# Masks of the first score block in quadrants, the mean's term and the constant rows on GpSimd, and new orders of work

## The chip, the cores and the metric

The kernel runs on one NeuronCore of a Trainium2 chip. The metric is the device time of one execution in microseconds (us). Five engines run their own instruction lists, each strictly in order, and meet only in semaphores: TensorE (PE in the profile, its weight loads PEld), VectorE (DVE), ScalarE (ACT), GpSimd (POOL) and SyncE (SP), which here only issues DMA transfers.

## The reference, cut to what matters

The input is x of shape 8 x 512 x 256: eight batches of 512 tokens. Each token is normalized, and two branches are added to x:

```python
xn = (x - mean(x)) / sqrt(var(x) + 1e-5)
# attention: 16 heads of 16, each token sees itself and the 63 before it
q, k, v = split(xn @ Wq), split(xn @ Wk), split(xn @ Wv)
attn = softmax(q . k_window / 4)            # tokens before the start are masked
a = (attn . v_window) @ Wo
# feed-forward with ternary weights (-1, 0, 1 by a threshold on |W|)
h = gelu(xn @ ternary(W_fc).T)              # 512 x 1024, exact gelu
h = (h - mean(h)) * rsqrt(var(h) + 1e-5) * ln_w + ln_b
f = h @ ternary(W_proj).T
out = x + a + f
```

## The kernel before, in words

All products run in fp16 or bf16 with each fp32 operand split into an upper and a lower half (`_hi`, `_lo`): ACT writes the upper half while it reads PSUM, DVE subtracts it from the PSUM value to get the lower. The second normalization is not applied to h. Instead the product of the raw gelu with `ln_w` goes through `W_proj`, and its result is scaled by the token's `rstd2`; what the subtracted mean contributes is a fixed row `csum[:, 0]` (the sum over W_proj of ln_w) times `mean2 * rstd2`, and the bias is a second fixed row `csum[:, 1]`, which GpSimd adds to x beforehand in `res`.

One batch is a set of jobs on TensorE, each with a PSUM tile of its own:

- `xt`: transposes of the normalized x. `qk` 0 and 1: queries and keys. `v`: values. `fc` 0 to 3: the hidden layer, one token tile of 128 each. `gt` 0 to 3: transposes of gelu. `proj` 0 to 3: the second layer.
- `sa` 0 to 7: scores of 64 queries with 128 keys for all 16 heads, queries on the partitions, only to find each row's maximum (DVE, line 691). `mt`: transpose of the maxima. They are split in two fp16 rows and copied into `q_stack` by DMA, so that the next product subtracts them.
- `st` 0 to 7: the same scores transposed, keys on the partitions, with the maximum subtracted. ACT reads each twice through exp: to `probs` (fp32, line 538) and to the fp16 `p_hi` (line 539). GpSimd subtracts to get `p_lo` (`lower_part`, line 429). `pv` 0 to 7: probabilities times values. DVE divides by the row sum (`scale_context`).
- `ct` 0 and 1: transposes of the context, `wo` 0 to 3: the output product.

`sa` and `st` need masks for the window. Each begins with a product of a one-hot matrix with a mask (lines 1002 and 1027) that starts the PSUM accumulation. `q_stack` and `k_stack` hold three parts of 16 rows per head on 48 of 64 partitions (two halves of the array, u = 0 and 1); 12 DMAs per batch fill them from `qk_split` (`load_stack`, line 330). `k_stack` also has constant rows of 256 and a zero block in front, written once at the start by DVE (`fill_stacks`, line 763).

The order of work is written out by hand for each engine. For TensorE it is the list `FIRST`, then `PERIOD` for p = 0, 1, ..., in which an entry (ahead, kind, n) is job n of batch p + ahead. PSUM tiles are handed out in that order: three large ones (`big`: xt, qk, v, fc, sa, st, gt) and two small ones (`small`: the rest), so that a job waits until the job three, or two, places before it in its ring has been read out (`wait_slot`). The probability buffers are three (`PB`), numbered by j % 3 in each batch: exp j waits for `pv` of j - 3. SyncE, GpSimd, ACT and DVE have such lists of their own, of calls `load_x`, `load_stack`, `shift_values`, `load_maxima`, `store`; `token_rstd` (the power for normalize, line 407), `residual` (line 423), `hidden_rstd` (line 414), `lower_part`; and so on. `add_projection` on DVE does two instructions for each token tile: rstd2 times `proj` plus `res` (line 727) and the mean's term (line 730).

Of the kernel before, what the change touches and what calls it, by code (L numbers as in the profile page):

```python
# [5 lines left out]
def attention_and_ternary_ffn(  # L6
# [30 lines left out]
    P = 128  # L37
# [18 lines left out]
    MAX_UNIT = 256.0  # L56

    ctx = ExitStack()
    with ctx:
# [80 lines left out]
        nrm2 = sb("nrm2", [P, NT], fp32)  # L140
        y_bufs = sb("y_bufs", [P, 3, NT, D], fp32)
# [66 lines left out]
        ffn_ready = event("ffn_ready", NT)  # L208
# [8 lines left out]
        res_ready = event("res_ready", 1)  # L217
        rstd_ready = event("rstd_ready", 1)
# [36 lines left out]
        def sig(name):  # L255
# [4 lines left out]
        FIRST = [(0, "wmax", 0), (0, "spread", 0), (0, "sums", 0), (0, "xt", 0), (0, "wmax", 1), (0, "sums", 1),  # L260
# [3 lines left out]
        PERIOD = [(0, "gt", 0), (0, "gt", 1), (0, "mt", 0), (-1, "pv", 5), (1, "qk", 0), (0, "gt", 2), (1, "qk", 1),  # L264
# [6 lines left out]
        ORDER = FIRST + [(p + ahead, kind, n) for p in range(NB + 4) for ahead, kind, n in PERIOD if 0 <= p + ahead < NB]  # L271

# [20 lines left out]
        def per_batch(operation):  # L293

            def of(b, *n):
                if 0 <= b < NB:
                    operation(b, *n)
            return of
# [5 lines left out]
        def _(sp):  # L304
# [7 lines left out]
            @per_batch  # L312
            def load_next_x(b):
                load_x(b + 1)

            @per_batch
            def load_stack(b, s, part):

                wait(sp, b, (qk_hi_ready, qk_ready)[part], s + 1)
                if s == 0 and part == 0:  # L320
                    if b >= 2:
                        wait(sp, b - 2, st_done, NJ)
                    else:
                        sp.wait_ge(stacks_filled, 1)
# [50 lines left out]
            load_ffn(1)  # L375
            copy_masks()
            for p in range(NB + 4):
                store(p - 4, 2)
                load_maxima(p - 2)
                shift_values(p - 2, 1)  # L380
                load_stack(p - 1, 0, 0)
                load_stack(p - 1, 0, 1)
                load_stack(p - 1, 1, 0)
                load_stack(p - 1, 1, 1)
                load_next_x(p - 1)
                shift_values(p - 1, 0)
                store(p - 4, 3)
                store(p - 3, 0)
                store(p - 3, 1)
# [5 lines left out]
        def _(pool):  # L395
# [30 lines left out]
            @per_batch  # L426
            def lower_part(b, j):
                wait(pool, b, p_hi_ready, j + 1)
                g.tensor_tensor(p_lo[:, j % PB], probs[:, j % PB], p_hi[:, j % PB], ALU.subtract).then_inc(  # L429
                    *sig(p_lo_ready))  # L430

            def constants():
# [10 lines left out]
                pool.wait_ge(onehot_ready, 1)  # L443

# [19 lines left out]
            constants()  # L464
            token_rstd(0)
            pads()
            masks()
            for p in range(NB + 4):
                token_rstd(p + 1)
                lower_part(p - 1, 3)  # L470
                lower_part(p - 1, 4)
                lower_part(p - 1, 5)
                residual(p)
                lower_part(p - 1, 6)
                lower_part(p - 1, 7)
                hidden_rstd(p)
                lower_part(p, 0)
                lower_part(p, 1)
                lower_part(p, 2)
# [3 lines left out]
        def _(act):  # L483
# [46 lines left out]
            @per_batch  # L530
            def exp(b, j):

                wait(act, b, st_done, j + 1)
                if j >= PB:

                    wait(act, b, pv_done, j - PB + 1)
                st = slot[b, "st", j][:].rearrange("p u (i q) -> p u i q", q=W)
                s.activation(probs[:, j % PB].rearrange("p i (u q) -> p u i q", u=2), st, ACT.Exp, scale=exp_scale[:, 0:1]).then_inc(*sig(exp_ready))  # L538
                s.activation(p_hi[:, j % PB].rearrange("p i (u q) -> p u i q", u=2), st, ACT.Exp, scale=exp_scale[:, 0:1]).then_inc(*sig(p_hi_ready))  # L539
# [30 lines left out]
            weight_upper(0)  # L570
            xt_upper(0)
            absolute(1)
            qk_upper(0, 0)
            qk_upper(0, 1)
            weight_upper(1)
            v_upper(0)
            gelu(0, 0)
# [5 lines left out]
            xt_upper(1)  # L583
            gelu_upper(0, 0)
            gelu_upper(0, 1)
            gelu_upper(0, 2)
            gelu_upper(0, 3)
            square(0, 2)
            qk_upper(1, 0)
            gelu_upper(0, 4)  # L590
            gelu_upper(0, 5)
            square(0, 3)
            for p in range(NB + 4):
                qk_upper(p + 1, 1)
                context_upper(p - 1, 0)
                gelu_upper(p, 6)
                gelu_upper(p, 7)
                exp(p, 0)
                v_upper(p + 1)
                exp(p, 1)  # L600
                exp(p, 2)
                gelu(p + 1, 0)
                gelu(p + 1, 1)
                exp(p, 3)
                exp(p, 4)
                gelu(p + 1, 2)
                square(p + 1, 0)
                gelu(p + 1, 3)
                context_upper(p - 1, 1)
                exp(p, 5)  # L610
                exp(p, 6)
                exp(p, 7)
                square(p + 1, 1)
                xt_upper(p + 2)
                gelu_upper(p + 1, 0)
                gelu_upper(p + 1, 1)
                gelu_upper(p + 1, 2)
                gelu_upper(p + 1, 3)
                square(p + 1, 2)
                qk_upper(p + 2, 0)  # L620
                gelu_upper(p + 1, 4)
                gelu_upper(p + 1, 5)
                square(p + 1, 3)
# [3 lines left out]
        def _(dve):  # L627
# [78 lines left out]
            def hidden_moments(b):  # L706
                wait(dve, b, square_ready, NT)
                link(v.scalar_tensor_tensor(out=msq[:], in0=gsum[:, 0], scalar=-1.0 / (HID * HID), in1=gsum[:, 0],
# [6 lines left out]
            @per_batch  # L715
            def hidden_scales(b):
                wait(dve, b, rstd2_ready, 1)
                v.tensor_scalar(rs2[:], rstd2[:], pow2[:, 4:5], None, ALU.mult)
                link(v.tensor_tensor(nrm2[:], mean2[:], rstd2[:], ALU.mult), b, moment_step, 3)

            @per_batch
            def add_projection(b, t):

                wait(dve, b, proj_done, t + 1)
                if t == 0:
                    wait(dve, b, res_ready, 1)
                v.scalar_tensor_tensor(out=y_ffn[:, b % 2, t], in0=slot[b, "proj", t][:, 0:D], scalar=rs2[:, t:t + 1],
                                       in1=res[:, t], op0=ALU.mult, op1=ALU.add).then_inc(*sig(proj_added))
                wait(dve, b, proj_added, t + 1)
                v.scalar_tensor_tensor(out=y_ffn[:, b % 2, t], in0=csum[:, 0], scalar=nrm2[:, t:t + 1],  # L730
                                       in1=y_ffn[:, b % 2, t], op0=ALU.mult, op1=ALU.add).then_inc(*sig(ffn_ready))
# [28 lines left out]

            def fill_stacks():

                link_pre(v.memset(k_stack[:], MAX_UNIT))
                v.memset(k_stack[:, :, :, 0:W], 0.0).then_inc(stacks_filled, 1)
# [76 lines left out]
            fill_stacks()  # L841
            statistics(0)
            weight_maxima(0)
            normalize(0)
            largest(0)
            scales(0)
            thresholds(0)
            weight_maxima(1)
            weight_lower(0)
            xt_lower(0)  # L850
            split_norm()
            thresholds(1)
            largest(1)
            ternary(1)
            qk_lower(0, 0)
            scales(1)
            qk_lower(0, 1)
            weight_lower(1)
            ternary(0)
            copy_row()  # L860
            v_lower(0)
            statistics(1)
            maximum(0, 0)
            maximum(0, 1)
            maximum(0, 2)
            normalize(1)
            maximum(0, 3)
            maximum(0, 4)
            maximum(0, 5)
            maximum(0, 6)  # L870
            maximum(0, 7)
            xt_lower(1)
            gelu_lower(0, 0)
            split_maxima(0)
            gelu_lower(0, 1)
            gelu_lower(0, 2)
            gelu_lower(0, 3)
            qk_lower(1, 0)
            gelu_lower(0, 4)
            copy_sums()  # L880
            gelu_lower(0, 5)
            qk_lower(1, 1)
            hidden_moments(0)
            gelu_lower(0, 6)
            gelu_lower(0, 7)
            hidden_scales(0)
# [261 lines left out]
```

## Time and profile before

| | |
|---|---|
| median of 3 runs | 439.74 us (438.87 to 441.53) |
| profiled execution | 440.41 us, its span 438.6 us |
| TensorE busy | 387.7 us, 88% |
| DVE busy | 348.8 us, 80% |
| ACT busy | 327.2 us, 75% |
| GpSimd busy | 182.5 us, 42% |
| mean granted TensorE clock | 0.984 |

The span goes from the first to the last instruction of the profiled execution; its own time is 1.8 us longer. Busy time is the union of an engine's instructions. A matmul's row shows its start and a modelled end, so consecutive ones overlap; the distance between starts is the better measure of their rate. Rows give, after the time, the engine, the line, the tiles out<-in and the shapes; "[... <-X]" is idle time before the instruction and what ended it.

### The profile page before, as it was taken

How to read it: one execution, taken by the hardware profiler on the slowest of the kernel's cores; microseconds unless marked ns; L12 is line 12 of the kernel's file. 1: busy time of each engine (PE TensorE's matmuls, PEld its weight loads, DVE VectorE, ACT ScalarE, POOL GpSimd, SP SyncE). 2: the span in 40 equal slices, each digit the busy share in tenths (PEclk: the TensorE clock that was granted, in tenths of full speed). 3: DMA queues.
4: the chain of work that ended last, by engine and by line, in shares of the span. 5: the costliest groups of instructions: out<-in, count | busy, mean ns of one | idle time of the engine just before them, and what ended most of it. 6: DMA issues, size and time to landing. Idle time of an engine off the chain costs nothing.

```text
span 438.6 us, 13237 instructions
## 1 busy us (share of the span) xinstructions
PE 387.7 (88%) x5692; PEld 266.4 (61%) x5692; DVE 348.8 (80%) x679; ACT 327.2 (75%) x407; POOL 182.5 (42%) x110
## 2 busy tenths in 40 slices
PE   0389699799999999899989999899989998898885
PEld 0236256466656677467656677567755766666674
DVE  7977687597887799589968899689958997669864
ACT  2234179868896788778897789778896889779861
POOL 2700003546163262437154344427244716335851
PEclk9999799999998999999999999999999999999999
DMA  7119207900392009700591029400880049001002
GB/s 272 63 42 121 67 3 99 141 3 1 67 120 57 14 29 129 124 13 17 91 150 24 13 58 128 95 13 28 119 133 16 1 92 120 22 13 50 16 31 67
DMA packets 30682, 29.19 MB, mean 67 GB/s; under 512 B 5664, under 2 KB 29280, under 8 KB 30624
## 3 DMA queue, kind: packets, MB, share of 16 engines
q1 hardware_dynamic: 30624, 28.35, 39.0%
q8 instruction: 45, 0.74, 0.8%
q14 instruction: 13, 0.11, 0.1%
HBM read 7.35 MB, written 4.19 MB: 26 GB/s over the span
## 4 chain that ended last, share of the span: by engine, by line
PE 37%; DVE 21%; SPq 17%; DMA 16%; issue 5%; ACT 3%; POOL 1%; POOLq 0%; DVEq 0%; ACTq 0%
SPq L330 12%; DMA x_in<-in_x 10%; PE small L1049 9%; PE big L989 7%; DMA k_stack<-qk_split 6%; DVE negmax L691 5%; PE big L963 3%; PE small L1060 3%; SPq L345 3%; PE big L1008 3%; PE big L1002 3%; DVE y_bufs L730 3%; PE small L1076 2%; DVE g_lo L685 2%; DVE ctxn L741 2%
## 5 line engine op out<-in xcount | busy, mean ns | idle before, releaser
L429 POOL TENSOR_TENSOR p_parts<-probs,p_parts 128x1024 f16<-128x1024 f32 x64 | 137.1, 2154 | 93.3 <-ACT p_parts L539 93.3
L538 ACT ACTIVATE probs<-big,exp_scale 128x1024 f32<-128x1024 f32 x64 | 71.5, 1117 | 29.9 <-PE big L1032 29.8
L691 DVE TENSOR_REDUCE negmax<-big 128x8 f32<-128x1024 f32 x64 | 77.1, 1221 | 7.6 <-PE big L1008 6.7
L539 ACT ACTIVATE p_parts<-big,exp_scale 128x1024 f16<-128x1024 f32 x64 | 71.5, 1117 | 0.0
L1049 PE MATMUL small<-proj_t,g_hi 128*128 128x256 f16 x256 | 59.2, 278 | 0.2 <-DVE ctxn L741 0.2
L1049 PE MATMUL small<-proj_t,g_lo 128*128 128x256 f16 x256 | 58.8, 276 | 0.0
L989 PE MATMUL big<-fc_t,xt_hi 128*128 128x512 f16 x128 | 49.8, 389 | 3.0 <-DVE negmax L691 2.8
L989 PE MATMUL big<-fc_t,xt_lo 128*128 128x512 f16 x128 | 49.5, 387 | 0.0
L516 ACT ACTIVATE gel<-big 128x1024 f32<-128x1024 f32 x32 | 32.7, 1024 | 20.9 <-PE big L989 20.2
L685 DVE SCALAR_TENSOR_TENSOR g_lo<-big,lnw_s,g_hi 128x512 f16<-128x512 f32 x64 | 44.9, 742 | 0.1
L553 ACT ACTIVATE g_hi<-big,lnw_s 128x512 f16<-128x512 f32 x64 | 39.6, 690 | 2.4 <-PE big L1039 2.3
L741 DVE TENSOR_TENSOR ctxn<-small,rden 64x128 f32<-64x128 f32 x128 | 36.9, 289 | 3.1
L1002 PE MATMUL big<-mask_q,onehot 64*128 64x512 bf16 x128 | 25.6, 395 | 14.0 <-DMA k_stack<-qk_split 12.4
L407 POOL TENSOR_TENSOR rstd<-veps,expo 128x4 f32<-128x4 f32 x8 | 8.1, 1010 | 68.6 <-DVE veps L652 68.6
L730 DVE SCALAR_TENSOR_TENSOR y_bufs<-csum,nrm,y_bufs 128x256 f32<-128x256 f32 x32 | 35.0, 1093 | 1.1
L646 DVE BATCH_NORM_STATS2 bn<-x_in 128x6 f32<-128x256 f32 x32 | 11.2, 411 | 30.1 <-DMA x_in<-in_x 30.1
L414 POOL TENSOR_TENSOR rstd<-var,expo 128x4 f32<-128x4 f32 x8 | 8.1, 1019 | 63.4 <-DVE var L713 63.4
L528 ACT ACTIVATE squares<-gel 128x1024 bf16<-128x1024 f32 x32 | 34.1, 1066 | 0.0
L1039 PE MATMUL big<-ident,gel 128*128 128x128 f32 x256 | 32.2, 273 | 0.1
L1039 PEld LDWEIGHTS big<-ident,gel 128*128 128x128 f32 x256 | 28.9, 141 | 2.1 <-DVE negmax L691 0.5
L1049 PEld LDWEIGHTS small<-proj_t,g_hi 128*128 128x128 f16 x256 | 25.4, 99 | 5.1 <-DVE ctxn L741 0.5
L1032 PEld LDWEIGHTS big<-q_stack,k_stack 50*128 50x128 f16 x1024 | 23.8, 95 | 7.6
(130 smaller groups left out, 833.5 us busy)
## 6 DMA issues: line engine op xcount, KB each, us to landing
q_stack<-qk_split SPq DMA_DIRECT2D x48, 128.0 KB, 4.7
k_stack<-qk_split SPq DMA_DIRECT2D x48, 128.0 KB, 7.5
x_in<-in_x SPq DMA_DIRECT2D x8, 512.0 KB, 9.3
out<-y_bufs SPq DMA_DIRECT2D x32, 128.0 KB, 1.8
v_odd<-v_even SPq DMA_DIRECT2D x16, 132.0 KB, 4.8
v_odd<-v_even SPq DMA_DIRECT2D x16, 99.0 KB, 4.7
gel<-in_w_fc SPq DMA_DIRECT2D x1, 1024.0 KB, 7.1
y_bufs<-in_w_proj SPq DMA_DIRECT2D x1, 1024.0 KB, 8.9
```

Source lines behind the costliest of these rows:

```text
L330: sp.dma_start(dst, qk_split[:, s, half, part]).then_inc(*sig(stacks_loaded[b % 2]))
L429: g.tensor_tensor(p_lo[:, j % PB], probs[:, j % PB], p_hi[:, j % PB], ALU.subtract).then_inc(*sig(p_lo_ready))
L538: s.activation(probs[:, j % PB].rearrange("p i (u q) -> p u i q", u=2), st, ACT.Exp, scale=exp_scale[:, 0:1]).then_inc(*sig(exp_ready))
L539: s.activation(p_hi[:, j % PB].rearrange("p i (u q) -> p u i q", u=2), st, ACT.Exp, scale=exp_scale[:, 0:1]).then_inc(*sig(p_hi_ready))
L553: s.activation(g_hi[:, i], slot[b, "gt", i // 2][:, i % 2], ACT.Copy, scale=lnw_s[:, i:i + 1]).then_inc(*sig(g_hi_ready))
L685: v.scalar_tensor_tensor(out=g_lo[:, i], in0=slot[b, "gt", i // 2][:, i % 2], scalar=lnw_s[:, i:i + 1], in1=g_hi[:, i], op0=ALU.mult, op1= ...
L691: v.tensor_reduce(negmax[:, :, j], slot[b, "sa", j][:].rearrange("p a (u k) -> p (a u) k", k=P), AX.X, ALU.max, negate=True).then_inc(*sig ...
L730: v.scalar_tensor_tensor(out=y_ffn[:, b % 2, t], in0=csum[:, 0], scalar=nrm2[:, t:t + 1], in1=y_ffn[:, b % 2, t], op0=ALU.mult, op1=ALU.ad ...
L741: last = v.tensor_tensor(ctxn[part, j], pv[part, :, a * DH:(a + 1) * DH], rden[part, j].unsqueeze(2).broadcast_to([W, NP, DH]), ALU.mult)
L989: last = mm(ps[:, a], xt[px][:, k, n * P:(n + 1) * P], fc_t[:, k, a * L:(a + 1) * L], start=(i == 0), stop=(i == 2 * KD - 1))
L1039: last = nc.tensor.transpose(ps[:, a, t * P:(t + 1) * P], gel[:, t, (2 * n + a) * P:(2 * n + a + 1) * P], ident[:])
L1049: last = mm(ps[:, 0:D], gt[pg][:, i, n * P:(n + 1) * P], proj_t[:, i], start=(i == 0 and pg == 0), stop=(i == NH - 1 and pg == 1))
```

## The change

Five things change.

1. In `sa` the mask product of each half u is done as two products of 64 by 64 (onehot rows u, one for each of the two output halves a), in the four-quadrant shape of the products that follow.
2. The mean's term leaves DVE. A new `add_mean` on GpSimd computes `nrm2`, then `mean_term = csum[:, 0] * nrm2`, then adds it to `res`; `add_projection` has one instruction and waits for it (`mean_added`). `hidden_moments` waits for the previous batch's `mean_step`.
3. The constant rows of `k_stack` are filled by GpSimd, one buffer after the other, as 32-bit words that hold two fp16 values; DVE's `fill_stacks` goes.
4. The probability buffers rotate by (b * 8 + j) % 3 across batches, and the first three exps of a batch wait for the last `pv` jobs of the batch before.
5. All five lists are new. The first batches and the last ones are written out, the period stands between. Within a batch, `qk` stands further ahead of `sa`, the four `fc` stand together, GELUs follow one another on ACT, `statistics` and `normalize` follow one another on DVE, and `load_x` stands before `load_stack` on SyncE. In the start DVE reduces both pairs of weights before it normalizes batch 0.

```diff
+        def fill_stacks():                       # GpSimd
+            for i in range(2):
+                step(g.memset(k_stack[:, i].bitcast(u32), MAX_UNIT_PAIR))
+                g.memset(k_stack[:, i, :, 0:W].bitcast(u32), 0).then_inc(stacks_filled, 1)
+                pool.wait_ge(stacks_filled, i + 1)
...
+        def add_mean(b):                         # GpSimd
+            wait(pool, b, rstd2_ready, 1)
+            wait(pool, b, res_ready, 1)
+            g.tensor_tensor(nrm2[:], mean2[:], rstd2[:], ALU.mult).then_inc(*sig(mean_step))
+            wait(pool, b, mean_step, 1)
+            g.tensor_tensor(mean_term[:], csum[:, 0:1, :].broadcast_to([P, NT, D]),
+                            nrm2[:].unsqueeze(2).broadcast_to([P, NT, D]), ALU.mult).then_inc(*sig(mean_step))
+            wait(pool, b, mean_step, 2)
+            g.tensor_tensor(res[:], res[:], mean_term[:], ALU.add).then_inc(*sig(mean_added))
...
         def add_projection(b, t):                # DVE
             wait(dve, b, proj_done, t + 1)
             if t == 0:
-                wait(dve, b, res_ready, 1)
+                wait(dve, b, mean_added, 1)
             v.scalar_tensor_tensor(... rs2 * proj + res ...)
-            wait(dve, b, proj_added, t + 1)
-            v.scalar_tensor_tensor(... csum[:, 0] * nrm2 + y_ffn ...)
...
         elif kind == "sa":                       # TensorE
             for u in range(2):
                 rows = slice(u * W, (u + 1) * W)
-                mm(ps[:, u], onehot[rows, 0:2].rearrange("p a q -> p (a q)"), mask..., start=True, stop=False)
+                for a in range(2):
+                    mm(ps[a * W:(a + 1) * W, u], onehot[rows, a], mask..., start=True, stop=False)
...
 # TensorE's period before, (ahead, kind, n) shortened to kind n [ahead]
-gt0 gt1 mt pv5[-1] qk0[1] gt2 qk1[1] pv6[-1] ct0[-1] gt3 st0 pv7[-1] v[1] st1 st2 wo3[-2] proj0 fc0[1] pv0
-fc1[1] sa0[1] st3 pv1 sa1[1] proj1 st4 pv2 sa2[1] fc2[1] pv3 sa3[1] wo0[-1] fc3[1] st5 ct1[-1] proj2
-sa4[1] proj3 st6 sa5[1] pv4 st7 wo1[-1] sa6[1] sa7[1] wo2[-1] xt[2]
 # and after, batches counted from the one whose proj it holds
+qk0[1] mt st7[-1] gt0 ct0[-1] pv4[-1] qk1[1] pv5[-1] pv6[-1] gt1 wo3[-2] gt2 pv7[-1] st0 v[1] wo0[-1] st1
+gt3 pv0 wo1[-1] st2 fc0[1] ct1[-1] proj0 fc1[1] fc2[1] sa0[1] fc3[1] sa1[1] pv1 sa2[1] sa3[1] st3 proj1
+xt[2] sa4[1] pv2 st4 proj2 sa5[1] st5 pv3 sa6[1] proj3 sa7[1] st6 wo2[-1]
 # TensorE's start after, up to batch 0's sa7
+wmax0 spread0 wmax1 spread1 sums0 xt sums1 qk0 qk1 fc0 fc1 v fc2 crow sa0 sa1 fc3 sa2 sa3 sa4 xt[1]
+sa5 sa6 csum sa7
 # GpSimd's period after
+lower3[-1] lower4[-1] lower5[-1] residual lower6[-1] hidden_rstd lower7[-1] lower0 lower1 token_rstd[2]
+add_mean lower2
```

## Rows read from the trace of the kernel before

**Rows 1.** The page, part 1: busy time, share of the span and instructions
```profile
PE 387.7 (88%) x5692; PEld 266.4 (61%) x5692; DVE 348.8 (80%) x679; ACT 327.2 (75%) x407; POOL 182.5 (42%) x110
```
**Rows 2.** By stretch: length, busy PE, PEld, DVE, ACT, POOL, granted clock, DMA share, GB/s
```profile
0.00:45.79 45.79, 24.42 (x132) 14.13 (x133) 34.35 (x56) 15.34 (x18) 10.83 (x23) 1.00 0.60 129
45.79:85.42 39.63, 32.54 (x366) 18.65 (x367) 27.96 (x48) 27.03 (x37) 10.91 (x6) 0.91 0.48 65
88.00:375.00 287.00, 273.74 (x4161) 190.67 (x4160) 237.92 (x474) 239.92 (x299) 129.57 (x66) 0.99 0.42 64
...
404.20:438.60 34.40, 26.86 (x491) 21.02 (x490) 23.61 (x59) 19.47 (x21) 18.07 (x9) 0.99 0.13 41
```
**Rows 3.** Waits over the span: total us, times, longest
```profile
PE big L1002 <- DMA k_stack<-qk_split: 12.4, 7, 2.9
```
**Rows 4.** TensorE's timeline: start, duration, at batch 5's first score block
```profile
279.19 0.39 PE L1002 MATMUL big<-mask_q,onehot 64*128 64x512 bf16 x2
```
**Rows 5.** TensorE's timeline of one `sa` block, the job behind it, and one `st` block
```profile
186.65 0.39 PE L1027 MATMUL big<-onehot,mask_k 64*128 64x512 bf16 x2 [0.69 <-DVE negmax L691]
186.87 0.40 PE L1032 MATMUL big<-q_stack,k_stack 50*128 50x64 f16 x16
...
188.09 0.39 PE L1002 MATMUL big<-mask_q,onehot 64*128 64x512 bf16 x2
188.41 0.42 PE L1008 MATMUL big<-k_stack,q_stack 48*64 48x128 f16 x16
188.76 0.39 PE L989 MATMUL big<-fc_t,xt_hi 128*128 128x512 f16 x1
```
**Rows 6.** Groups by line: shapes, count, busy us, mean ns, idle before
```profile
L730 DVE SCALAR_TENSOR_TENSOR y_bufs<-csum,nrm,y_bufs 128x256 f32<-128x256 f32 x32 | 35.0, 1093 | 1.1
L423 POOL TENSOR_TENSOR res<-x_in,csum 128x1024 f32<-128x1024 f32 x8 | 20.1, 2513 | 19.9 <-issue 19.9
L414 POOL TENSOR_TENSOR rstd<-var,expo 128x4 f32<-128x4 f32 x8 | 8.1, 1019 | 63.4 <-DVE var L713 63.4
L691 DVE TENSOR_REDUCE negmax<-big 128x8 f32<-128x1024 f32 x64 | 77.1, 1221 | 7.6 <-PE big L1008 6.7
L516 ACT ACT_TABLE_LOAD x15 | 19.2, 1283 | 0.3
```
**Rows 7.** The chain that ended last: first `qk` product of the kernel, and `qk` 1 of batch 5
```profile
24.37 4.66 PE big L963 x12
...
260.37 2.59 PE big L963 x12
```
**Rows 8.** Timelines of DVE and GpSimd, the same stretch of each, columns as in rows 4
```profile
237.33 0.48 DVE L730 SCALAR_TENSOR_TENSOR y_bufs<-csum,nrm,y_bufs 128x256 f32<-128x256 f32 x1
248.57 1.72 DVE L730 SCALAR_TENSOR_TENSOR y_bufs<-csum,nrm,y_bufs 128x256 f32<-128x256 f32 x1
268.30 2.12 POOL L429 TENSOR_TENSOR p_parts<-probs,p_parts 128x1024 f16<-128x1024 f32 x1 [0.99 <-ACT p_parts L539]
268.90 1.56 DVE L718 TENSOR_SCALAR rs<-rstd,pow 128x4 f32<-128x4 f32 x1
```
**Rows 9.** The page, part 6, DMA issues: count, KB each, median us from issue to landing
```profile
k_stack<-qk_split SPq DMA_DIRECT2D x48, 128.0 KB, 7.5
x_in<-in_x SPq DMA_DIRECT2D x8, 512.0 KB, 9.3
...
probs<-in_w_o SPq DMA_DIRECT2D x1, 256.0 KB, 7.4
```
**Rows 10.** Timeline of the start, DVE and SyncE's queue
```profile
2.72 7.74 DVE L763 MEMSET k_stack<- 128x9216 f16 x1 [2.72 <-issue]
3.29 0.47 SPq L355 DMA_DIRECT2D probs<-in_w_o  x1
...
14.21 3.10 DVE L660 TENSOR_SCALAR xn<-x_in,mv,rstd 128x256 f32<-128x256 f32 x4
```
**Rows 11.** The chain that ended last, near its end
```profile
427.74 2.10 POOLq L59
```

More of the change, by code:

```diff
@@ L375, in _ @@
             load_ffn(1)
-            copy_masks()
[L377 to L389, printed above, removed]
+            load_x(1)
@@ L390, in _ @@
+            store(7, 2)
+            store(7, 3)
             for t in range(NT):
@@ new lines, in _ @@
+            exp(0, 0)
+            v_upper(1)
+            exp(0, 1)
+            gelu_upper(0, 6)
+            gelu_upper(0, 7)
+            exp(0, 2)
+            gelu(1, 0)
+            gelu(1, 1)
+            gelu(1, 2)
+            square(1, 0)
+            gelu(1, 3)
+            square(1, 1)
+            exp(0, 3)
+            xt_upper(2)
+            exp(0, 4)
+            square(1, 2)
+            exp(0, 5)
+            square(1, 3)
+            exp(0, 6)
+            qk_upper(2, 0)
+            gelu_upper(1, 0)
@@ new lines, in _ @@
+            gelu_upper(6, 4)
+            gelu_upper(6, 5)
+            exp(6, 0)
+            v_upper(7)
+            exp(6, 1)
+            gelu_upper(6, 6)
+            gelu_upper(6, 7)
+            exp(6, 2)
+            context_upper(5, 1)
+            gelu(7, 0)
+            gelu(7, 1)
+            square(7, 0)
+            gelu(7, 2)
+            gelu(7, 3)
+            square(7, 1)
+            exp(6, 3)
+            exp(6, 4)
+            square(7, 2)
+            exp(6, 5)
+            square(7, 3)
@@ L626, in _ @@
+            exp(7, 6)
+            exp(7, 7)
+            context_upper(7, 1)
         @block.vector
@@ new lines, in _ @@
+            statistics(2)
+            normalize(2)
+            scale_context(0, 0)
+            maximum(1, 0)
+            maximum(1, 1)
+            add_projection(0, 0)
+            maximum(1, 2)
+            maximum(1, 3)
+            scale_context(0, 1)
+            add_projection(0, 1)
+            maximum(1, 4)
+            xt_lower(2)
+            scale_context(0, 2)
+            add_projection(0, 2)
+            maximum(1, 5)
+            maximum(1, 6)
+            scale_context(0, 3)
@@ new lines, in _ @@
+            scale_context(0, 7)
+            hidden_scales(1)
+            v_lower(2)
+            scale_context(1, 0)
+            add_attention(0, 1)
+            gelu_lower(1, 6)
+            gelu_lower(1, 7)
+            statistics(3)
+            normalize(3)
+            maximum(2, 0)
+            context_lower(0, 1)
+            maximum(2, 1)
+            add_projection(1, 0)
+            maximum(2, 2)
+            maximum(2, 3)
+            scale_context(1, 1)
+            add_projection(1, 1)
@@ new lines, in _ @@
+            normalize(4)
+            maximum(3, 0)
+            context_lower(1, 1)
+            maximum(3, 1)
+            add_projection(2, 0)
+            maximum(3, 2)
+            maximum(3, 3)
+            scale_context(2, 1)
+            add_projection(2, 1)
+            maximum(3, 4)
+            xt_lower(4)
+            scale_context(2, 2)
+            add_projection(2, 2)
+            maximum(3, 5)
+            maximum(3, 6)
+            scale_context(2, 3)
+            add_projection(2, 3)
@@ new lines, in _ @@
+            add_attention(4, 0)
+            hidden_scales(5)
+            v_lower(6)
+            scale_context(5, 0)
+            add_attention(4, 1)
+            gelu_lower(5, 6)
+            gelu_lower(5, 7)
+            statistics(7)
+            normalize(7)
+            maximum(6, 0)
+            context_lower(4, 1)
+            maximum(6, 1)
+            add_projection(5, 0)
+            maximum(6, 2)
+            maximum(6, 3)
+            scale_context(5, 1)
+            add_projection(5, 1)
```

618 lines of the change are left out of this document (483 added, 135 removed), and 56 rows, old and new, of tables (FIRST, LAST, PERIOD).

## The prediction

> **What bounds the kernel now.** I read the engines' shares first: TensorE is busy 88% of the span, DVE, the next, 80% [rows 1]. Then a table by stretch. From 88 to 375 us lie six batches of 47.8 us; TensorE works 273.7 of the 287 us, 45.6 a batch, DVE 39.7, ACT 40.0, GpSimd 21.6 [rows 2]. So a batch costs what TensorE's jobs cost plus 2.2 us, 13.3 us of idle in all six. The waits say what most of that is: the first score block (kind `sa`) waits for the stacked keys, 12.4 us over 7 batches, 2.9 at worst, in batch 1 [rows 3]. At both ends TensorE is not the limit: 21.4 of the first 45.8 us and 7.1 of the next 39.6 are idle, and after pauses there TensorE is granted only the lower level, 1.2 GHz, instead of 2.4, for some us: the mean clock of that second stretch is 0.91 [rows 2].
>
> **Part 1, masks.** Alone, a score block goes: masks start, first product 0.32 us later, next job 0.35 us after that [rows 5]. The second-pass block (`st`), whose masks and products have the same tile shape, needs 0.22 to 0.23 us from masks to products [rows 5]. So changing the tile shape costs 0.10 us; I take the same for the joints between jobs, which no row isolates. The change makes masks and products one shape. Counted over both job lists the shape changes 285 times before and 219 after: the 64 inside the blocks go, the joints between jobs save 2 net. 66 x 0.10 = 6.6 us. Are four masks of 512 columns as quick as two? No row has them. Upper bound: column halves in series, 0.43 instead of 0.32, +0.11 us a block. Lower: 0.22. I take 0.22, because 16 products of 128 columns in four quadrants would take 0.43 us in two series and take 0.35 with the shape change in it. About 1 us of the 6.6 falls where DVE's maxima set the pace. **-5.6.**
>
> **Part 2, mean's term.** Per batch DVE loses four additions, 1.09 us each on average, and one small product: 39.7 goes to 35.2 us a batch [rows 2, 6]. DVE does not set the batch, so this pays only through slack. GpSimd gains three instructions in series: a 128x4 product (from nearly nothing to 1.02 as its power of that size; I take 1.0, its own engine's row), a 128x1024 product (2.12 like its subtraction; both operands repeat, so up to twice the addition's 2.51; I take 2.5) and a 128x1024 addition (2.5) [rows 6, 8]. 6.0 us, bounds 4.3 to 8.6; GpSimd goes from 21.6 to 27.6 of 46 us. Behind it on GpSimd waits the third probability block of the batch; TensorE has `proj`, three `fc`, four `sa` and a value product before it wants that one, over 10 us, so **0**; without that cover up to 6 us a batch. Three waits are new. The first addition of a batch's `proj` waits for the mean's term, with the next maxima queued behind it on DVE: the term starts when the power for normalize is done, and DVE has normalize, two maxima and a lowering, 4.5 us, and TensorE about 9 before that addition. The moments wait for the previous batch's term, half a batch old by then. A batch's first three exponentials wait for value products 5 to 7 of the batch before, which TensorE's list now has ahead of their `st` blocks. All **0**.
>
> **Part 3, order in the steady stretch.** From the end of the second `qk` product to the first `sa` block it is now 262.96 to 279.19 us, 16.2, in a batch with 0.9 of waiting: the stacks need 16.2 and TensorE has 15.3 of work [rows 4, 7]. The new list puts between them, beside the old jobs or their like, two more `gt`, one more `fc`, two `wo` and one `pv`: about 1.8 + 1.7 + 1.3 + 0.6 = 5.4 us. 20.7 of cover against 16.2: the wait goes; next in line are waits for a maximum before a `st` block, of some 0.5 us. The x load moves ahead of the stack transfers on SyncE's queue (12 issues of 0.65 us, landing after 7.5) and needs `res` of two batches before; from last `proj` to the statistics TensorE has about 20 us of jobs, the load needs 0.5 + 2.1 + 2.5 + 9.3 = 14.4 [rows 6, 8, 9]. Stores now stand between the stack transfers and the copies of maxima on SyncE, the last of them two batches old and its `wo` done before the `mt` that the maxima need: 0. ACT keeps its four GELUs together: of 31 table loads of 1.28 us, 15 for GELU, some 16 stay: 19 us off ACT, 37.4 of 46 us a batch [rows 6]. Of the 13.3 us idle, 9.5 are the stack waits without the first; they go; the 3.8 left I raise to 5.8 for waits of the new order. **-7.5.** Bounds: -12 (all gone) and +1 (as many new ones).
>
> **Part 4, start.** DVE's 7.74 us fill of `k_stack` goes [rows 10]. It is not all gain: DVE now also reduces the second weight pair before normalizing, and w_o, issued at 3.3, lands 7.4 later, at 10.7 [rows 9]. So: 10.7 + 1.2 (maximum) + 1.4 (scales, largest) = 13.3; normalize 1.6 to 3.1 (four at 0.41, stretched to 3.1 beside GpSimd's fills; I take 2.3) [rows 10]; transposes 2.0; ACT 1.0; DVE 1.2; first `qk` product at 20 instead of 24.4. `qk` 4.7 + 2.6 gives 27.3 [rows 7]; twelve stack issues run from 25.7 to 33.5, the last lands 7.5 later, 41 [rows 9]. The constant row comes by another chain at the same time: ternary 3.6 us after the norm's parts ends at 35, 5.4 us of products give 40.4. First `sa` block at 40.5 to 41, instead of 45.79. GpSimd's fills (no row: 2304 elements, 2.0 by the slope of its fills, 3.6 by the 0.20 us for 128) end by 18 for batch 0, wanted at 25.7. **-5.0**, bounds -2 to -8.
>
> **Part 5, first batch.** From the first `sa` to batch 1's: 39.6 us, 7.1 idle, and a mean clock 0.09 below full costs another 3.5 (0.09 x 39.6) [rows 2]. Now DVE's eight maxima (1.22 each [rows 6]) and one 1.2 us lowering still pace the score blocks, 11 us, but the `qk` product runs inside them. I leave 2 us idle there and 3 before the first value product, which has exp, 1.3 of table and 2.1 of GpSimd before it: 5 instead of 7.1; of the 3.5 I give back 2.5. **-4.6**, bounds 0 to -9.
>
> **Part 6, end.** 34.4 us from batch 7's first `st` block to the end, in which ACT works 19.5 [rows 2]. Now the exponentials (8 x 2.23) with two scalings 1.3 and two copies 1.2 go through, then 2.1 on GpSimd and 8.8 from there to the end (429.8 to 438.6) [rows 11]: 1.1 + 17.8 + 2.5 + 2.1 + 8.8 = 32.3. GpSimd, with the mean's term just before, ends its eight at the same moment. **-2.0**, bounds +1 to -4.
>
> Sum: 5.6 + 7.5 + 5.0 + 4.6 + 2.0 = 24.7 us. The profiled execution took 440.4 (span 438.6 and 1.8 around it); 415.7. It lies 0.7 above the median of the runs, so **415** on their scale.
>
> **Rivals.**
> *DVE locked out by GpSimd.* The addition that leaves DVE takes 0.48 us with GpSimd idle and 1.72 beside a GpSimd addition; the 128x4 scaling takes 1.56 us and ends as GpSimd's subtraction does [rows 8]. So what reads SBUF twice, or scales SBUF to SBUF, stands still until GpSimd is through. In the new order normalize comes right behind the power, and the three instructions of the mean's term start beside it: it could take 6.0 instead of 1.4 us. The Trainium skill (SBUF — State Buffer, "Who interferes with whom") states this as a rule: DVE's second SBUF port is GpSimd's only one, and whoever issues first holds it for the whole instruction; it speaks against putting more work on GpSimd, and the trace agrees: 1.72 against 0.48. By the rows DVE would be at 39.8 us a batch, still under 46, but 4.6 us late just before the maxima; TensorE has 9 us of jobs from the last `gt` to `sa`, DVE 10 to do. Late by 1 to 3 us: at 2 a batch, 7 x 2 = 14, 429. For: the rows. Against: the removed additions were the most blocked. 0.07.
> *The order brings its own waits.* Idle stays at 2.2 us a batch: 415 + 7.5 = 422.5. For: three queues hold long in-order lists. 0.16.
> *Masks in series.* 64 x 0.21 = 13 more: 428. 0.04.
> *All cover holds.* Bounds of parts 3 to 6 half way: 405 to 408. 0.16.
> *Slower: x lands late.* The power for batch p+2 stands on GpSimd ahead of the mean's term and of the third probability block, and it waits for x. If x and the twelve stack transfers share bandwidth so that x lands 10 us later, then 24.4 against 20 stops GpSimd for 4.4, and with it value products and exponentials, 7 times. From 3.5 us late on the gain is eaten; at 6 us late: 415 + 42 = 457. For: the DMA engines are busy 0.42 of that time, and the transfers come together [rows 2]. Against: x now goes first. 0.04.
> *The head does not move* (weights land as before and bound it) and orders trade evenly: no change, 438. 0.02.
>
> **Numbers.** The forecast has 0.51; 1% (4.4 us) is about what a measurement can tell. Faster: 0.51 + 0.07 + 0.16 + 0.04 + 0.16 = 0.94, of which I move 0.01 to no change: 0.93; same 0.03; slower 0.04. Range 405 to 430: it takes in all but the slow case, no change, and the outer parts of the all-cover case and of the lock.
>
> **What would show it.** Masks: 0.22 us from masks to products; if 0.43, part 1 fails. Batches 45.8 to 46.5 us apart; no wait of `sa` on `k_stack` after the first; DVE waits for x under 5 us. First `sa` at 41. GpSimd 230 us busy. Normalize at 1.4 us, or 6 if the lock bites. TensorE share 91 to 92%. Wrong would be: batches at 48, or a GpSimd queue that waits for the statistics while value products stand.

## The result, and the profile after

The changed kernel takes 449.49 us (median of 4 runs, 445.45 to 450.49) against 440.27 (438.87 to 441.53) for the kernel before on the same chip: a ratio of 1.018, 95% interval 1.0141 to 1.0219. It is slower by 1.8%, with an interval clear of 1; the forecast was 415 us, and the time lies outside its range of 405 to 430.

The page of the changed kernel, parts 1 and 2 (of part 2 the clock), and the table by stretch (length, busy PE, PEld, DVE, ACT, POOL, clock, DMA share, GB/s), to hold against [rows 1, 2]:

```profile
PE 391.7 (88%) x5820; PEld 276.2 (62%) x5820; DVE 355.8 (80%) x637; ACT 309.0 (69%) x393; POOL 220.6 (49%) x138
PEclk9999899989998999989996999879996999998899
88.00:375.00 287.00, 269.00 (x4161) 192.29 (x4162) 244.96 (x427) 212.26 (x269) 145.26 (x78) 0.95 0.37 60
```

Two things are strange. DVE is busier than before, though 35 us of additions [rows 6] have left it. And in the steady stretch, where the forecast left TensorE 5.8 us of idle time, it has 18.0 of 287 us against 13.3 before, and its mean clock is 0.95 instead of 0.99. What DVE is busy with stands in the groups (count, busy us, mean ns of one, idle before; first the kernel before, then the changed one), what TensorE waits for in the waits (total us, times, longest):

```profile
L660 DVE TENSOR_SCALAR xn<-x_in,mv,rstd 128x256 f32<-128x256 f32 x32 | 12.7, 460 | 0.1
L943 DVE TENSOR_SCALAR xn<-x_in,mv,rstd 128x256 f32<-128x256 f32 x32 | 47.4, 1542 | 8.8 <-POOL rstd L509 8.8
```
```profile
PE small L1563 <- DVE ct_lo L1029: 14.8, 6, 3.2
PE big L1505 <- DMA mask_k<-mask_k: 3.7, 1, 3.7
```

Normalize (four instructions a batch) took 12.7 us in the whole kernel before and takes 47.4 now. These 34.7 us are as much as the additions had freed, but that is chance, as more than these two terms changed. The fill (7.7 us) is gone as well, and the two 128x4 instructions `msq` and `var` of the hidden layer's moments took 1.5 and 1.3 us before and take 9.1 and 14.5 now. The new order puts them beside `residual` and a probability block on GpSimd, and this `var` (0.16 us before) ends when the block that runs from 256.99 to 259.12 does:

```profile
257.09 2.05 DVE L995 SCALAR_TENSOR_TENSOR var<-gsum,msq 128x4 f32<-128x4 f32 x1
```

One batch of normalize, the timelines of GpSimd, DVE and TensorE over the same microseconds (start, duration):

```profile
280.03 0.20 POOL L533 TENSOR_TENSOR nrm<-mean,rstd 128x4 f32<-128x4 f32 x1
280.31 2.02 POOL L535 TENSOR_TENSOR mean_term<-csum,nrm 128x1024 f32<-128x1024 f32 x1
282.41 2.35 POOL L538 TENSOR_TENSOR res<-res,mean_term 128x1024 f32<-128x1024 f32 x1
284.72 2.18 POOL L543 TENSOR_TENSOR p_parts<-probs,p_parts 128x1024 f16<-128x1024 f32 x1
```
```profile
280.17 6.88 DVE L943 TENSOR_SCALAR xn<-x_in,mv,rstd 128x256 f32<-128x256 f32 x4 [1.19 <-POOL rstd L509]
286.97 1.21 DVE L974 TENSOR_REDUCE negmax<-big 128x8 f32<-128x1024 f32 x1
288.10 0.68 DVE L1029 TENSOR_TENSOR ct_lo<-small,ct_hi 128x512 f16<-128x512 f32 x1
```
```profile
285.59 0.40 PE L1511 MATMUL big<-k_stack,q_stack 48*64 48x128 f16 x16
288.83 0.86 PE L1563 MATMUL small<-v_even,p_parts 128*128 128x33 f16 x24 [2.85 <-DVE ct_lo L1029]
289.63 0.64 PE L1505 MATMUL big<-mask_q,onehot 64*64 64x512 bf16 x4
290.06 0.64 PE L1511 MATMUL big<-k_stack,q_stack 48*64 48x128 f16 x16
```

Read them together. Normalize starts at 280.17 and ends at 287.05; the four GpSimd instructions run from 280.03 to 286.90. The row puts four instructions together. Asked for in windows that hold one at a time, they are:

```profile
280.17 0.41 DVE L943 TENSOR_SCALAR xn<-x_in,mv,rstd 128x256 f32<-128x256 f32 x1 [1.19 <-POOL rstd L509]
280.49 1.99 DVE L943 TENSOR_SCALAR xn<-x_in,mv,rstd 128x256 f32<-128x256 f32 x1
282.40 2.51 DVE L943 TENSOR_SCALAR xn<-x_in,mv,rstd 128x256 f32<-128x256 f32 x1
284.83 2.21 DVE L943 TENSOR_SCALAR xn<-x_in,mv,rstd 128x256 f32<-128x256 f32 x1
```

The first takes its usual 0.41 us. The other three end at 282.48, 284.91 and 287.04, each 0.14 to 0.15 us after one of the three long GpSimd instructions (282.33, 284.76, 286.90): DVE gets through one instruction for each of GpSimd's. A maximum and the lowering of the context (`ct_lo`) are queued behind it on DVE. The value product needs the PSUM slot that the lowering reads, so TensorE stands still for 2.85 us. After the pause the products take 0.64 us instead of 0.40, at the lower of the clock's two levels. The windows around it give the granted clock as a mean, 0.50 in the five microseconds from 289:

```profile
280.00:286.00 6.00, 5.99 (x63) 2.63 (x60) 5.83 (x4) 4.76 (x9) 5.84 (x5) 1.00 0.04 13
286.00:289.00 3.00, 0.17 (x6) 0.17 (x7) 3.00 (x4) 2.89 (x5) 0.90 (x1) 0.89 0.00 0
289.00:294.00 5.00, 5.00 (x90) 3.50 (x88) 4.35 (x7) 1.44 (x2) 0.00 (x0) 0.50 0.01 3
294.00:298.00 4.00, 4.00 (x66) 3.11 (x66) 1.31 (x2) 1.70 (x2) 2.13 (x1) 0.85 0.00 0
```

Normalize starts at 80.49, 129.80, 179.27, 229.23 and 280.17 in five successive batches: 49.9 us a batch instead of 47.8.

### The profile page after: what moved, and what is told of

Its sections match the earlier page's. It is cut to its first block, busy times and chain, and to the rows that moved or that the text cites. A ratio compares the mean times of both kernels' runs of the same rounds, so it can differ in the third digit from the quotient of the medians.

```text
span 447.2 us, 13502 instructions
## 1 busy us (share of the span) xinstructions
PE 391.7 (88%) x5820; PEld 276.2 (62%) x5820; DVE 355.8 (80%) x637; ACT 309.0 (69%) x393; POOL 220.6 (49%) x138
## 4 chain that ended last, share of the span: by engine, by line
PE 50%; DVE 28%; issue 7%; POOL 5%; ACT 5%; DMA 3%; SPq 1%; POOLq 0%; DVEq 0%
PE small L1552 12%; DVE xn L943 9%; PE big L1465 6%; PE small L1563 6%; PE big L1477 4%; PE big L1505 4%; POOL p_parts L543 4%; DVE var L995 3%; PE big L1530 3%; DVE negmax L974 3%; PE big L1491 3%; PE big L1511 3%; DVE qk_split L955 3%; PE small L1579 3%; DVE g_lo L968 2%
## 5 line engine op out<-in xcount | busy, mean ns | idle before, releaser
L974 DVE TENSOR_REDUCE negmax<-big 128x8 f32<-128x1024 f32 x64 | 77.0, 1221 | 23.3 <-PE big L1511 22.4
L1552 PE MATMUL small<-proj_t,g_hi 128*128 128x256 f16 x256 | 65.0, 294 | 1.5 <-issue 1.4
L1552 PE MATMUL small<-proj_t,g_lo 128*128 128x256 f16 x256 | 64.4, 292 | 0.0
L943 DVE TENSOR_SCALAR xn<-x_in,mv,rstd 128x256 f32<-128x256 f32 x32 | 47.4, 1542 | 8.8 <-POOL rstd L509 8.8
L736 ACT ACTIVATE g_hi<-big,lnw_s 128x512 f16<-128x512 f32 x64 | 41.1, 688 | 12.1 <-PE big L1542 12.1
L698 ACT ACTIVATE gel<-big 128x1024 f32<-128x1024 f32 x32 | 32.7, 1023 | 21.9 <-PE big L1491 21.8
L1563 PE MATMUL small<-v_even,p_parts 128*128 128x33 f16 x768 | 25.0, 180 | 17.8 <-DVE ct_lo L1029 14.8
L1563 PEld LDWEIGHTS small<-v_even,p_parts 128*128 128x128 f16 x768 | 22.5, 97 | 21.8 <-DVE ct_lo L1029 15.7
L1542 PE MATMUL big<-ident,gel 128*128 128x128 f32 x256 | 35.4, 285 | 0.2 <-DVE g_lo L968 0.2
L1505 PE MATMUL big<-mask_q,onehot 64*64 64x512 bf16 x256 | 28.5, 435 | 4.9 <-DMA mask_k<-mask_k 3.7
L1552 PEld LDWEIGHTS small<-proj_t,g_hi 128*128 128x128 f16 x256 | 26.9, 105 | 8.1 <-issue 1.9
L525 POOL TENSOR_TENSOR res<-x_in,csum 128x1024 f32<-128x1024 f32 x8 | 18.8, 2355 | 22.0 <-issue 22.0
```

What stands on the lines that cost most here:

```text
L736: s.activation(g_hi[:, i], slot[b, "gt", i // 2][:, i % 2], ACT.Copy, scale=lnw_s[:, i:i + 1]).then_inc(*sig(g_hi_ready))
L943: last = v.tensor_scalar(xn[:, t], x_in[:, b % 2, t], mv[:, t, 0:1], rstd[:, t:t + 1], ALU.subtract, ALU.mult)
L974: v.tensor_reduce(negmax[:, :, j], slot[b, "sa", j][:].rearrange("p a (u k) -> p (a u) k", k=P), AX.X, ALU.max, negate=True).then_inc(*sig ...
L1505: mm(ps[a * W:(a + 1) * W, u], onehot[rows, a], mask_q[rows, 1 if n == 0 else 0].rearrange("p u k -> p (u k)"), start=True, stop=False)
L1542: last = nc.tensor.transpose(ps[:, a, t * P:(t + 1) * P], gel[:, t, (2 * n + a) * P:(2 * n + a + 1) * P], ident[:])
L1552: last = mm(ps[:, 0:D], gt[pg][:, i, n * P:(n + 1) * P], proj_t[:, i], start=(i == 0 and pg == 0), stop=(i == NH - 1 and pg == 1))
```

## The experiments

**Theory.** GpSimd's mean term holds back normalize, what is queued behind it makes TensorE pause, and the pause costs clock besides. **Rivals.** The new order costs by itself; four small masks are slow; the term is too much for GpSimd wherever it stands; the late mask copies at the start upset what follows. Each ratio is to the kernel before, run again beside the experiment: its median was 440.4 us beside experiments 1 to 4, 441.0 beside 5 to 8 and 440.2 beside 9.

**1. The mean's term waits until normalize is done.** Nothing is left out or added but a wait:

```diff
         def add_mean(b):
+            if b + 2 < NB:
+                wait(pool, b + 2, xn_ready, 1)
```

> The changed kernel, with one wait more: GpSimd starts the mean's term of batch b only when DVE has normalized batch b + 2. Theory (lock): normalize falls from 6.9 to 1.4 us a batch, TensorE's pause of 2.9 us before the second value product of each batch goes and with it some 2 us a batch at the lower clock; 6 x 5 = 30 us less than the changed kernel's 449: 415 to 425. Rival (order): the pause comes from where the context's lower half and its PSUM tile stand in the new lists; normalize is short and the pause stays: 440 to 449. A third: the term now comes 1.4 us later and DVE waits for it before the first addition; 425 to 435.

Measured: **417.85 us**, ratio 0.950 [0.944, 0.956], 31.6 us less than the changed kernel. One wait turns 1.8% slower into 5% faster. Its normalize group, GpSimd beside one normalize, and the steady stretch:

```profile
L945 DVE TENSOR_SCALAR xn<-x_in,mv,rstd 128x256 f32<-128x256 f32 x32 | 14.7, 523 | 8.8 <-POOL rstd L509 8.8
```
```profile
264.35 1.38 DVE L945 TENSOR_SCALAR xn<-x_in,mv,rstd 128x256 f32<-128x256 f32 x4 [1.19 <-POOL rstd L509]
```
```profile
263.24 1.01 POOL L509 TENSOR_TENSOR rstd<-veps,expo 128x4 f32<-128x4 f32 x1 [1.97 <-DVE veps L937]
265.82 0.20 POOL L535 TENSOR_TENSOR nrm<-mean,rstd 128x4 f32<-128x4 f32 x1 [1.57 <-DVE xn L945]
```
```profile
88.00:375.00 287.00, 284.31 (x4649) 204.70 (x4647) 234.98 (x454) 238.52 (x306) 163.88 (x89) 1.00 0.38 63
```

GpSimd gives up 1.6 us a batch and TensorE gets 4.7 back: the same five normalizes as above (83.61 to 264.35) are now 45.2 us apart on average. Idle falls from 18.0 to 2.7 us, the clock is at 1.00. GpSimd does the same work as in the changed kernel (219.9 us busy), so it is not the amount of it.

**2. The mean's term stays on DVE,** all else as changed: `add_mean` and its waits go, `add_projection` has its second instruction again.

> The changed kernel with the mean's term back on DVE as before the change (two instructions for each token tile). Theory (lock): GpSimd has only the subtraction of a probability block beside normalize, which falls from 6.9 to 3 or 4 us; the additions take 1.1 us each on DVE again, which is hidden; most of the pause goes: 420 to 430. Rival (order): no change from 449, or slower by DVE's 4.4 us a batch more, up to 460.

Measured: **426.83 us**, ratio 0.969 [0.963, 0.975]. Everything in the change but the move of the term is worth 14 us; the move then costs 23 as the change does it, and gains 9 with the wait of experiment 1. In this kernel TensorE waits six times for another lowering on DVE (`xt_lo`, 7.1 us in all) and is busy for 276.51 us of the steady stretch. Two things hold DVE up there, and no run parts them: the additions are back (29.1 us), and a normalize still takes 3.1 us in the steady batches beside the one probability block (23.3 us in all, 14.7 in experiment 1). So the 9 us are not shown to be the additions' alone.

**3. Only the masks, in the old order.**

```diff
-    mm(ps[:, u], onehot[rows, 0:2].rearrange("p a q -> p (a q)"), mask..., start=True, stop=False)
+    for a in range(2):
+        mm(ps[a * W:(a + 1) * W, u], onehot[rows, a], mask..., start=True, stop=False)
```

> The kernel before with the score block's masks in 64 by 64 products, nothing else. By the forecast's part 1: 64 drains of 0.10 us less, 5 to 7 us faster, 433 to 435. If column halves ran in series: 6 to 7 us slower. If TensorE only waits longer for the stacked keys: 0 to -3.

Measured: **438.93 us**, ratio 0.9947 [0.9912, 0.9981] (10 runs): by the ratio 2.3 us, not 6. Where the rest goes is open. The profiled execution is the slowest of the ten (443.99 us), so its rows can only hint: the wait of the first score blocks for the stacked keys is as before (12.4 us in 7), and the waits for maxima before `st` blocks are 3.5 us against 1.8.

**4. The masks are copied at the start, ahead of the work on the values,** in the changed kernel. On SyncE the two mask copies stood behind the shifts of the values:

```diff
+            copy_masks()     # right behind load_x(1)
...
-            copy_masks()     # was behind shift_values
```

> The changed kernel with the two mask copies issued before the stack transfers of batch 0 instead of behind the first values' shift. Theory: the first score block waits 3.7 us for the copy of the key mask because the copies sit late in the queue; it now starts with the constant row's products done, at 42.6 instead of 46.3: 3 to 4 us faster, 445 to 446. Rival: it then waits for the stacks, which land at the same time: no change.

Measured: **442.65 us**, ratio 1.0056 [1.0021, 1.0092] (10 runs), 7 under the changed kernel, twice what was expected. The 3.7 us wait for the copy is gone, and the first score block starts at 42.98 instead of 46.34. But the start differs between executions of the same list as well: with the late copies that block starts at 46.34 in the changed kernel and at 47.56, 46.60, 44.67 and 43.11 in experiments 1, 6, 7 and 8. Counted from the first `qk` product it comes 23.5 to 24.8 us later in these five traces, and 22.1 and 21.6 in the two with early copies (this one and 5). So the copies are worth about 2 us of the 7; the rest is not explained.

**5. Both: the wait of 1 and the early copies of 4.**

> Both edits that helped together: GpSimd's mean's term waits for normalize, and the mask copies go out before batch 0's stack transfers. If they are independent: 418 less 4 to 7 = 411 to 414. Rival: the earlier start is given back in the first batch, where the maxima pace the score blocks: 416 to 418.

Measured: **414.5 us** (411.45 to 415.77), ratio 0.938 [0.932, 0.945], the fastest of all and faster than both kernels. The waits of TensorE's that remain are under 2.5 us each but for the weights' at the start. Its stretch from 88 us:

```profile
88.00:375.00 287.00, 281.99 (x4569) 202.83 (x4567) 235.90 (x459) 237.36 (x303) 164.56 (x89) 1.00 0.40 64
```

**6. Experiment 1 with the old masks.**

> The kernel of the first experiment (the mean's term waits for normalize) with the score block's masks as before, two products of 64 by 128. Here TensorE is busy nearly all the time, so drains should count in full: 72 more changes of the tile shape, 291 instead of 219, of 0.10 us: 7 us slower than 417.9, 423 to 426. If masks in quadrants are worth only what they brought in the old order (2 us): 420.

Measured: **425.86 us**, ratio 0.9645 [0.958, 0.971]. Against experiment 1 the new masks are worth 8.0 us. The two kernels have TensorE busy 285.46 and 284.31 of the 287 us: where nothing else bounds, the shape change is paid in full.

**7. Work in the place of the pause.** In the changed kernel, score block 1 is computed six times over from batch 2 on, ahead of the place where TensorE stands still; the repeats give the same values. Each repeat is 0.44 us, so that it is some 13 us more work, and it keeps TensorE busy while DVE is held back:

```diff
+    for again in range(6 if n == 1 and b >= 2 else 1):
         ...   # masks and products of sa 1
```

> The changed kernel; in batches 2 to 7 TensorE does the second score block six times over, with the same result, right before the value product that waits 2.9 us. It is 2.2 us of work more a batch, laid in the pause; DVE, which is still normalizing, does not need the block sooner. Theory (the pause also costs the clock): without a pause the granted clock stays at the upper level and some 2 us a batch come back: 5 x 2 = 10 us faster than the changed kernel's 449, 436 to 442. Rival (only the wait itself counts): no change, 447 to 451. If the repeats do not fit in the pause: slower, up to 460.

Measured: **440.32 us**, ratio 0.997 [0.992, 1.001] (10 runs): 9 us less than the changed kernel with 13 us more to do. Normalize is still stretched, but the waits are short and the clock stays up. The profiled execution is the fastest (436.34 us); over all ten the mean clock is 0.981 to 0.992, against 0.954 to 0.961 in the four of the changed kernel.

```profile
L943 DVE TENSOR_SCALAR xn<-x_in,mv,rstd 128x256 f32<-128x256 f32 x32 | 45.8, 1490 | 8.8 <-POOL rstd L509 8.8
```
```profile
PE small L1564 <- DVE ct_lo L1029: 3.7, 6, 1.0
```
```profile
88.00:375.00 287.00, 280.67 (x4816) 202.01 (x4812) 248.37 (x433) 222.66 (x283) 154.15 (x83) 0.99 0.39 63
```

The same five normalizes are 48.6 us apart, against 49.9 in the changed kernel and 45.2 in experiment 1.

**8. The mean's term ahead of the power for normalize** in GpSimd's list.

```diff
-            token_rstd(p + 4)
             add_mean(p + 2)
+            token_rstd(p + 4)
```

> The changed kernel with one exchange in GpSimd's list, no wait added: the mean's term of batch b stands ahead of the power for batch b + 2 instead of behind it. Theory (lock): the term runs in GpSimd's idle time before the statistics; normalize meets only one probability block, 2.1 us, and takes 3 to 4 us, but starts 1 to 3 us later, since the power waits for the term: 420 to 430. Rival (order): 445 to 450.

Measured: **429.32 us**, ratio 0.971 [0.963, 0.980]. Normalize is shorter (21.1 us in all, mean 718 ns) but starts later: DVE waits 20.3 us for the power in the kernel instead of 8.8. TensorE's waits for the lowering are 8.8 us in 6, 2.0 at most. Two thirds of the loss against experiment 1 are gone. What stays goes with both: the later start (11.5 us more waiting in the whole kernel) and the stretch that is left (6.4 us more).

**9. Only the mean's term moved, in the kernel before:** between the first and the second `lower_part` of the old order.

```diff
             lower_part(p, 0)
+            add_mean(p)
```

> The kernel before, with the mean's term alone moved to GpSimd, between the two probability blocks of the old order; old masks, old SyncE order, old starts and ends. Theory (it is the place beside the normalize that costs, not the move): here the three GpSimd instructions do not stand beside a normalize whose result TensorE's next score block needs, so the normalize stays near the 460 ns of L660 of before or under 700, VectorE is rid of 35 us of additions, and the time is 436 to 441, little or no gain, as TensorE sets the steady batches at 2.4 GHz. Rival (any move of this term to GpSimd costs time, by the lock or by GpSimd's later probability blocks): 445 to 455, with the wait before the first addition of the output product over 2 us in each batch.

Measured: **448.0 us**, ratio 1.018 [1.0145, 1.0212]. The expectation fails; the rival's time holds, and half its mechanism. Normalize is at 459 ns, untouched. Its last one starts at 338.5 us against 337.6 before, so up to there the move costs 0.9 us, and the 25 us that have left DVE's stretch (212.89 busy, to hold against [rows 2]) gain nothing. The loss is behind that: the profiled execution, the slowest of the five (450.99 us), has its last `st` masks 9.6 us later than the kernel before. Both groups of these masks from 337 us on (count: shortest, median, longest ns, first and last start), then the last batch's timeline on GpSimd, TensorE's waits from 375 us on, and its windows:

```profile
L1027 PE MATMUL big<-onehot,mask_k x38: 378/387/387, 337.9 to 424.0; 64*128 64x512 bf16 x38
L1040 PE MATMUL big<-onehot,mask_k x38: 378/387/607, 338.8 to 433.6; 64*128 64x512 bf16 x38
```
```profile
411.06 2.13 POOL L443 TENSOR_TENSOR p_parts<-probs,p_parts 128x1024 f16<-128x1024 f32 x1 [1.03 <-ACT p_parts L554]
413.14 0.21 POOL L433 TENSOR_TENSOR nrm<-mean,rstd 128x4 f32<-128x4 f32 x1
413.43 1.90 POOL L435 TENSOR_TENSOR mean_term<-csum,nrm 128x1024 f32<-128x1024 f32 x1
415.40 2.34 POOL L438 TENSOR_TENSOR res<-res,mean_term 128x1024 f32<-128x1024 f32 x1
417.70 6.29 POOL L443 TENSOR_TENSOR p_parts<-probs,p_parts 128x1024 f16<-128x1024 f32 x3
```
```profile
PE small L1073 <- POOL p_parts L443: 6.8, 3, 4.9
```
```profile
375.00:380.00 5.00, 4.85 (x83) 3.02 (x84) 2.75 (x5) 2.15 (x3) 0.83 (x2) 0.50 0.02 5
415.00:420.00 5.00, 0.15 (x10) 0.06 (x3) 1.18 (x4) 2.12 (x2) 4.92 (x4) 0.92 0.00 1
420.00:425.00 5.00, 5.00 (x58) 3.44 (x58) 1.27 (x4) 0.00 (x0) 3.99 (x2) 0.50 0.01 3
```

In the last batch no `fc` and `sa` jobs cover the 4.5 us that the term puts ahead of the probability blocks: TensorE has 0.15 busy us in five, and then 5 us at the lower level. That is 6.3 of the 9.6 us. The other 3.3 are there before the term of the last batch: `st` masks that stand 1.6 us later than before at 376.26 stand 3.7 later at 382.19, after a wait of 2.6 us that was followed by the lower level.

## Why the prediction was wrong

The starts of the first score block, of batch 1's, of batch 7's first `st` block and the end of the span, from TensorE's timelines, give four parts. The forecast's are from its parts 4, 5, 2 to 3 with the masks, and 6:

| us | before | forecast | changed | experiment 5 |
|---|---|---|---|---|
| to the first score block | 45.8 | 41 | 46.3 | 44.5 |
| to that of batch 1 | 39.6 | 35.0 | 36.4 | 36.7 |
| to batch 7's first `st` | 318.8 | 305.7 | 330.5 | 300.2 |
| to the end | 34.4 | 32.4 | 33.9 | 32.7 |
| span | 438.6 | 414.1 | 447.2 | 414.0 |

**Part 2 failed,** in its "All 0", and with it the rival that spoke for it. It looked at what waits for the mean's term, and not at what runs beside it. The rival *DVE locked out by GpSimd* named the place and nearly the size of the stretch (6.0 us instead of 1.4; it is 6.9, as the probability block behind the term joins in). Its row of 1.72 us stood beside a probability block's subtraction (247.89 to 250.02) and not beside an addition, which takes nothing from it. It got a chance of 0.07 and a price of 14 us; experiment 1 puts the price at 31.6. The 0.07 rested on "the removed additions were the most blocked", which compares totals on an engine that doesn't bound. The 14 took 2 us a batch from a count of work, 9 us on TensorE against 10 on DVE up to the maxima. It left out that a value product waits for the lowering queued behind one maximum, a pause of 2.9; and that the pause costs clock. Per batch, against experiment 1, it is 49.9 - 45.2 = 4.7 us. Idle gives 2.7 of it (18.0 us over 5.75 batches of 49.9 against 2.7 over 6.35 of 45.2); the 2.0 left fit the clock, 0.95 against 1.00. Experiment 7, which fills the pause and so takes away the clock's part alone, gets 1.3 a batch back.

That it is GpSimd's use of the port and not its load, nor its queue, is shown by the same work in another place (1, 8) and by DVE's share coming back with it. That pause and clock carry the cost, and not the stretch as such, is shown by experiment 7: normalize takes the same 6 to 7 us, and 13 us of added work are more than paid for. The Trainium skill (SBUF — State Buffer, "Who interferes with whom") has the rule that VectorE's second port is GpSimd's only one and is held for a whole instruction; the trace agrees, with normalize's end at 287.05 as the fourth GpSimd instruction ends at 286.90. The rule spoke against this change, was cited, and was then outvoted. The four rows of one instruction each, above, show the turns: the last three wait for one GpSimd instruction each. The forecast also passed over the moments, which its new order put beside GpSimd's `residual`. They lose 20.8 us of DVE's time (`msq` and `var` together) in the changed kernel and as much in experiment 1, where TensorE has 2.7 us idle in the steady stretch: there it costs little.

**Part 1, masks,** held: 0.24 us from masks (282.95) to products (283.19), with 0.22 forecast and 0.43 for the rival *masks in series*. Worth 8.0 us where TensorE bounds (5.6 forecast), 2.3 in the old order. What the part left open is how much the saving depends on the rest.

**Part 3, order,** held: the steady waits for stacked keys are gone, DVE waits for x 4.6 us in all, table loads fell from 31 to 17. In experiment 1 batches of 45.2 us stand beside 45.8 to 46.5 forecast. The middle came out 5.5 us better than forecast in experiment 5, 2.4 of it by the masks. *Slower: x lands late* did not happen: x landed 5.1 us after its issue, not 9.3.

**Part 4, start,** failed twice. Normalize starts at 13.51 (13.3 forecast) but takes 4.92 us, not 2.3, as GpSimd fills the constant rows beside it; the first `qk` product then starts at 22.8, not at 20. And I passed over the mask copies queued behind the shifts of values on SyncE: TensorE waits 3.7 us for them, of which experiment 4 puts about 2 to their account. This is the timeline of the start of the changed kernel, DVE, GpSimd and SyncE's queue:

```profile
13.51 4.92 DVE L943 TENSOR_SCALAR xn<-x_in,mv,rstd 128x256 f32<-128x256 f32 x4
```
```profile
13.36 2.02 POOL L562 MEMSET k_stack<- 128x2304 uint32 x1
15.44 0.35 POOL L563 MEMSET k_stack<- 128x256 uint32 x1
15.84 2.05 POOL L562 MEMSET k_stack<- 128x2304 uint32 x1
17.95 0.34 POOL L563 MEMSET k_stack<- 128x256 uint32 x1
```
```profile
37.21 0.60 SPq L378 DMA_DIRECT2D v_odd<-v_even  x1
37.85 0.60 SPq L409 DMA_DIRECT2D mask_q<-mask_q  x1
38.49 0.60 SPq L410 DMA_DIRECT2D mask_k<-mask_k  x1
```

The copy of `mask_k`, issued at 38.49, releases the first score block at 46.34. With it out of the way (5) the block starts at 44.49, 3.5 us behind the forecast; the late `qk` product accounts for 2.8 of it. No run keeps the fills off normalize on purpose, but the trace of experiment 8, whose list of the start is the same, has it so. There normalize was ready before them:

```profile
12.75 1.36 DVE L943 TENSOR_SCALAR xn<-x_in,mv,rstd 128x256 f32<-128x256 f32 x4
```

The fills start at 14.62, the first `qk` product at 19.19, and the first score block at 43.11, still with its 3.7 us of waiting. So the stretch is worth some 3 us of the start, and whether it comes about differs from one execution to the next.

**Parts 5 and 6** were near: 36.7 against 35.0, and 32.7 against 32.4. The sizes of the small steps: the mean's term is 0.20 + 1.9 to 2.0 + 2.35 = 4.5 us, not 6.0 (the 128x4 product costs a fifth of the power).

That experiment 5 lands on the forecast (414.5 against 415) is partly luck: the middle was 5.5 better, the start 3.5, the first batch 1.7 and the end 0.3 worse. And it is not the kernel that was forecast, but that kernel with two repairs.

## What to carry to other kernels

When work moves to GpSimd, list what DVE runs in the same microseconds and, behind that, what TensorE waits for; the price is the lateness of that chain, not either engine's busy time. One wait that keeps GpSimd's block off a critical SBUF-to-SBUF instruction of DVE can be worth far more than it costs. Then check the last batch apart, where the jobs that cover such a block are missing.

## What the hardware showed that was not expected

- After a pause of 2.85 us TensorE worked 5 us at 0.50 of its clock; in experiment 7, with waits of at most 1.0 us in the same place, it kept 0.99 over the steady stretch. Other pauses of near that length went either way: at batch 7's first score block the kernel before waited 2.3 us and kept 1.00, experiment 9 waited 2.6 us and had 0.50 for the next five.
- Beside a chain of GpSimd instructions DVE got one SBUF-to-SBUF instruction through for each of GpSimd's, 0.14 to 0.15 us after it ended. An instruction of 128x4, 0.16 us by itself, took 2.05. The maxima, which read PSUM, kept their 1.22 us in every kernel here.
- GpSimd memsets, which read nothing, stretched DVE's normalize too: 4.92 us for four instructions that take 1.4 alone. It goes the other way as well: in experiment 8 a memset that takes 0.30 us in the changed kernel (`mask_q`, 64x256) took 1.49, as normalize had started 0.12 us before it.
- GpSimd does a product of 128x4 in 0.20 us, and its power of the same size in 1.02.
